# Perceiver attention on one core: context preparation over five pairs, and a table load placed after the square roots

## The chip, the cores and the metric

One core of a Trainium2 chip (trn2). The metric is device time in microseconds (us), the median of the runs shown; the profile describes one further execution of the same program. TensorE does the matrix products, VectorE (DVE) and ScalarE (ACT) the elementwise work, GpSimd (POOL) a part of the normalisation, and SyncE (SP) issues the transfers.

## The reference

Four residual steps run one after the other on x, of shape 8 x 100 x 512: a perceiver cross attention, a mixture of experts (4 experts, two per token), a strided cross attention and a second mixture of experts (8 experts, two per token), each scaled by tanh of a gate. The change lies in the first step alone:

```python
xn = layernorm(x, ln_x_g, ln_x_b)            # x: the context rows, 8 x 722 x 512
ln = layernorm(latents, ln_l_g, ln_l_b)      # latents: layernorm of x, 8 x 100 x 512
q = ln @ Wq                                  # 16 heads of 64
kv = concatenate((xn, ln), axis=1) @ Wkv     # 822 keys and values per batch
sim = where(mask, (q * scale) @ k.T, -max)
out = softmax(sim) @ v                       # per head
out = layernorm(out @ Wout, ln_o_g, ln_o_b)
```

## The kernel before

`perceiver_attention` (line 59) goes through 8 batches, and in each through 8 pairs of heads (index `i` for the batch, `hp` for the pair, `n = 8 i + hp`). Each engine has its own instruction stream, written out by hand in the same loop order, and the streams meet only in semaphores. There is no planner: the order in which TensorE works is the order in which the loops at lines 797 to 832 issue.

One turn of TensorE, pair n: the scores of pair n (`scores`, 690), the attention product of pair n-2 (`attend`, 717), then in alternation the transposes of pair n-1's probabilities (`transposes`, 705) and the keys of pair n+1 (`keys`, 673), and at the end the *extras* of the pair (`extras`, 241). Extras are tiles of two kinds. A *values tile* ("v") is 12 products of 512 columns into one PSUM bank, which ScalarE copies to `v_sb` (515). A *context tile* ("in") is 4 transposes of 128 normalised context rows of the next batch into one PSUM bank (637); ScalarE copies the high part out (497) and VectorE writes the low part (883), and only then is the bank free. Twelve values tiles and six context tiles are needed per batch. The first four values tiles of a batch are made in the last two pairs of the batch before (`NEXT`), the rest in its own pairs (`OWN`; `FIRST_OWN` for batch 0). `PREP` says how many context tiles of the next batch each pair makes. Within a pair the two kinds alternate, values first (253).

Keys, values and context tiles share two PSUM banks (`kv_ps`), which are handed out in strict turns: each use takes the other bank than the use before it, and `wait_kv` (624) makes TensorE wait until the use before last has been read out. So a context tile behind one values tile waits for the second part of the keys, whose bank VectorE frees with `k_lo` (900); a context tile right behind another context tile waits for ScalarE's copy of the values tile before both.

ScalarE's stream of one pair (584 to 609) is: `move_t` of the first transposes (533), high keys part 0 (526), `move_t` of the second, `exponent` of head 0 (543), high keys part 1, `exponent` of head 1, at pairs 0 and 2 a square root (`deviations`, 489), then the copies of the extras. TensorE's second round of transposes waits for the first `move_t`, since both use the bank `t_ps`. The square root at pair 0 is for the next batch's context rows, the one at pair 2 (from batch 1 on) for the output of the batch before; in the last batch there is one more at pair 5. A square root and an exponential need different activation tables; the compiler puts an ACT_TABLE_LOAD ahead of the first activation that needs the other table. The copies need neither.

VectorE's stream of one pair (1027 to 1076): at pair 1 it takes the reciprocal of the deviations and normalises the first three context tiles, at pair 2 the other three, at pair 3 it finishes the output of the batch before (`finish`, 944); then `move_o` (927), `move_t` (920), the maximum and division of both heads, the low keys (900) between them, and the low parts of the pair's context tiles. GpSimd multiplies and adds gain and bias to each normalised context tile (461, 462), and TensorE's context tile waits for that. SyncE loads the rows of batch i+2 once the last context tile of batch i+1 has been transposed (430).

Of the kernel before, what the change touches and what calls it, by code (L numbers as in the profile page):

```python
# [8 lines left out]
ACT = mybir.ActivationFunctionType  # L9
# [49 lines left out]
def perceiver_attention(nc, ctx_rows, x_in, keep_mask, ln_x_g, ln_x_b, ln_l_g, ln_l_b, wq, wkv, wout,  # L59
# [5 lines left out]
    B, M, D = x_in.shape  # L65
    N = ctx_rows.shape[1]
    P = 128
# [28 lines left out]
    with ExitStack() as ctx:  # L96
        def sb(name, shape, dt=F32, where=ctx):
            return where.enter_context(nc.sbuf_tensor("a_" + name, shape, dt))
# [47 lines left out]
        eps = sb("eps", [P, 1])  # L146
        ident = sb("ident", [P, P])
        stats = sb("stats", [P, CT + 2, 6])
        mean_var = sb("mean_var", [P, CT + 2, 2])
        std = sb("std", [P, CT + 2])  # L150
        rstd = sb("rstd", [P, CT + 2])
        l_stats = sb("l_stats", [P, B, 6])
# [79 lines left out]
        pool_chain = sem("pool_chain")  # L232

        halves = (slice(0, HD), slice(HD, P))
        OWN = [2, 1, 2, 1, 1, 1, 0, 0]
        FIRST_OWN = [4, 3, 2, 1, 1, 1, 0, 0]
        NEXT = [0, 0, 0, 0, 0, 0, 2, 2]
        PREP = [0, 0, 0, 2, 2, 2, 0, 0]
        P_FROM = [sum(PREP[:hp]) for hp in range(PAIRS)]

        def extras(i, hp):

            own = OWN if i else FIRST_OWN
            first = VS - sum(own[hp:])
            vs = [("v", i, v) for v in range(first, first + own[hp])]
            if i + 1 < B:
                first = sum(NEXT[:hp])
                vs += [("v", i + 1, v) for v in range(first, first + NEXT[hp])]
            ins = [("in", i + 1, t) for t in range(P_FROM[hp], P_FROM[hp] + PREP[hp]) if i + 1 < B]
            both = []  # L250
            if (i, hp) == (0, 0):
                both = [("tail", u) for u in range(TAILS)]
            while vs or ins:
                both += vs[:1] + ins[:1]
                vs, ins = vs[1:], ins[1:]
            return both

        def turned(i, hp):

            return [j for j, at in ((i - 2, 1), (i - 1 if i == B - 1 else -1, 7)) if j >= 0 and hp == at]  # L260
# [220 lines left out]
        def _(act):  # L481
# [3 lines left out]
            def deviations(first, end):  # L485

                dev[0] += 1
                act.wait_ge(var_done, dev[0])
                nc.scalar.activation(std[:, first:end], mean_var[:, first:end, 1], ACT.Sqrt, bias=eps[:, :]).then_inc(std_done, 1)
# [31 lines left out]
            def keys(n, part):  # L521
                c, w = PART[part]
                act.wait_ge(k_ready, 2 * n + part + 1)
                if n:
                    act.wait_ge(s_ready, 2 * n)
                nc.scalar.activation(k_hi[:, c:c + w], kv_bank("k", n, part)[:, 0:w], ACT.Copy).then_inc(k_hi_done, 1)  # L526

            def move_t(n, x):
                a, b = ROUND[0]
                act.wait_ge(t_ready, 4 * n + 2 * x + 1)  # L530
                if n:
                    act.wait_ge(o_ready, n)
                nc.scalar.activation(probs_t[:, x, M * a:M * b], t_ps[:, 0:M * (b - a)], ACT.Copy).then_inc(ta_done, 1)  # L533

            def move_next(b):
                act.wait_ge(xt_ready, b + 1)
                if b:
                    act.wait_ge(routed, b)
                nc.scalar.activation(xn_t[:, :, :], turn_bank(b).rearrange("p (k q) -> p k q", q=P)[:, :, 0:M], ACT.Copy).then_inc(turn_sem(b), 1)

            def exponent(n, x):
                act.wait_ge(max_done, 2 * n + x + 1)
                nc.scalar.activation(probs[0:M, x, 0:KEYS], probs[0:M, x, 0:KEYS], ACT.Exp, scale=-1.0,  # L543
                                     bias=neg_max[0:M, x:x + 1], accum_out=row_sum[0:M, x:x + 1]).then_inc(exp_done, 1)
# [39 lines left out]
            for i in range(B):  # L584
                for hp in range(PAIRS):
                    n = PAIRS * i + hp
                    if n:
                        move_t(n - 1, 0)
                    if n + 1 < PAIRS * B:
                        keys(n + 1, 0)  # L590
                    if n:
                        move_t(n - 1, 1)
                    exponent(n, 0)
                    if n + 1 < PAIRS * B:
                        keys(n + 1, 1)
                    for j in turned(i, hp):
                        move_next(j)
                    exponent(n, 1)
                    if hp == 0:
                        if i + 1 < B:  # L600
                            deviations(0, CT + 1)
                        else:
                            deviations(NEXT_IN, NEXT_IN + 1)
                    if hp == 2 and i:
                        deviations(OUT, OUT + 1)
                    if hp == 5 and i == B - 1:
                        deviations(NEXT_IN, NEXT_IN + 1)
                    for kind, *at in extras(i, hp):
                        {"v": values, "in": prepare, "tail": tail_values}[kind](*at)
            move_t(PAIRS * B - 1, 0)  # L610
            move_t(PAIRS * B - 1, 1)
            deviations(OUT, OUT + 1)
# [1938 lines left out]
def flamingo_layers(nc, x, ctx_1024, mask_BxS2_bk0, g_xattn, g_ffn,  # L2551
# [11 lines left out]
    with ExitStack() as ctx:  # L2563
        logits = ctx.enter_context(nc.sbuf_tensor("logits", [P, B * m_wg_t.shape[1]], F32))
        route1 = RoutingAhead(nc, "f", ctx, x.shape, f_router_w, f_router_b, logits)
        route2 = RoutingAhead(nc, "m", ctx, x.shape, m_wg_t, None, logits)
        gates = ctx.enter_context(nc.sbuf_tensor("gates", [P, B, TOP], F32))
        with nc.cleanup_on_exit():
            perceiver_attention(nc, ctx_1024, x, mask_BxS2_bk0, a_ln_x_g, a_ln_x_b, a_ln_l_g, a_ln_l_b, a_wq, a_wkv, a_wout,
                                a_ln_o_g, a_ln_o_b, g_xattn[0:1], x1, route1)  # L2570

        least = -(-B * M * TOP // P)
        even = m_wg_t.shape[1] * -(-B * M * TOP // m_wg_t.shape[1] // P)
        with nc.cleanup_on_exit(), ExitStack() as held:
            rows_at = held.enter_context(nc.sbuf_tensor("f_rows_at", [P, 2, slots(B * M, f_router_b.shape[0])], mybir.dt.uint32))
            with ExitStack() as early:
                tensors = ExpertTensors(nc, "f", early, B, B * M, D, f_router_b.shape[0], least + least % 2, False)
            ahead = ContextAhead(nc, held, (tensors.wab_hi, tensors.wab_lo, tensors.x_hi, tensors.x_lo), B, B * M, g_ctx, g_wk_t, g_wv_t)
            with ExitStack() as early:
                sums = SumsAhead(nc, early, ahead, rows_at, x1, y1, least + least % 2)  # L2580
            with nc.cleanup_on_exit():
                gated_experts(nc, "f", x1, route1, f_pieces, g_ffn[0:1], gates, y1, None, least + least % 2, tensors, ahead, sums)
            strided_attention(nc, x1, y1, gates, ahead, sums, g_wq_t, g_bias, g_wo_t, g_bo, g_xattn[1:2], x3, route2)
        with nc.cleanup_on_exit():
            gated_experts(nc, "m", x3, route2, m_pieces, g_ffn[1:2], gates, y2, out, even)
# [57 lines left out]
```

## Time and profile before

| | us |
|---|---|
| median of 3 runs | 2108.15 |
| lowest and highest run | 2107.41, 2115.01 |
| span of the profiled execution | 2099.3 |
| TensorE busy in the span | 1928.3 (92%) |
| VectorE, ScalarE, GpSimd busy | 1026.6, 845.0, 657.1 |

The span goes from the first to the last instruction. The profile gives no other time for that execution; the runs shown lie 8.1 to 15.7 us above the span, for what is outside it. The eight batches of the perceiver lie between about 110 and 1060 us; the three later stages follow.

### The profile page before, as it was taken

The page shows a single profiled execution, that of the slowest core. Times are in us where ns is not written, and L with a number is a line of the kernel's source. Part 1 is how long each engine was busy: PE and PEld are TensorE (multiplying, and loading weights), DVE is VectorE, ACT ScalarE, POOL GpSimd, SP SyncE. Part 2 cuts the span into 40 slices and gives each one's busy share as a digit, 9 for nine tenths or more (in the row PEclk, how much of TensorE's full clock was granted, in tenths as well). Part 3 has the DMA queues.
Part 4 walks back from the last instruction along what each step waited for, and adds up shares of the span by engine and source line. Part 5 has one row for each costly group of instructions (what it writes and reads, how often), then busy time and mean ns, then how long its engine had stood idle before and what let it go on. Part 6 is the DMA issues. An engine that isn't in the chain of part 4 may idle for free. (4 is left out here: it accounts for less than half of the span.)

```text
span 2099.3 us, 35633 instructions
## 1 busy us (share of the span) xinstructions
PE 1928.3 (92%) x12328; PEld 1568.3 (75%) x12328; DVE 1026.6 (49%) x2245; ACT 845.0 (40%) x1792; POOL 657.1 (31%) x551
## 2 busy tenths in 40 slices
PE   4889999999999999999859999999997895999994
PEld 3577878777777878787748888888885675999983
DVE  6324555555555555544464233333336566554564
ACT  3233443444434434334435233333322544555550
POOL 4011020303020110300023455554433204688872
PEclk9899999999999999999969999999998996999997
DMA  7630101010110201000044233333348216454546
GB/s 209 200 130 1 53 15 53 19 53 11 37 35 9 63 9 53 19 17 18 5 152 137 57 110 110 105 110 120 109 143 263 101 58 202 147 200 152 209 146 202
DMA packets 113526, 201.58 MB, mean 96 GB/s; under 512 B 33135, under 2 KB 33935, under 8 KB 112867
## 3 DMA queue, kind: packets, MB, share of 16 engines
q1 hardware_dynamic: 108579, 183.94, 27.3%
q0 software_dynamic: 4800, 15.73, 2.3%
q8 instruction: 86, 1.41, 0.3%
q14 instruction: 61, 0.50, 0.1%
HBM read 171.65 MB, written 27.99 MB: 95 GB/s over the span
## 5 line engine op out<-in xcount | busy, mean ns | idle before, releaser
L461 POOL TENSOR_TENSOR a_rows<-a_rows,a_gain_x 128x512 f32<-128x512 f32 (+1 forms) x48 | 69.3, 1443 | 555.7 <-DVE a_rows L876 555.7
L620 PE MATMUL a_kv_ps<-a_kvin_hi,a_wk_hi 128*128 128x512 f32 (+1 forms) x512 | 196.0, 383 | 1.0 <-DVE a_kvin_lo L883 1.0
L1094 PE MATMUL f_banks<-f_wab_hi,f_x_hi 128*128 x448 | 183.8, 410 | 0.7 <-DVE f_x_lo L1781 0.7
L621 PE MATMUL a_kv_ps<-a_kvin_lo,a_wk_hi 128*128 128x512 f32 (+1 forms) x512 | 180.3, 352 | 0.0
L622 PE MATMUL a_kv_ps<-a_kvin_hi,a_wk_lo 128*128 128x512 f32 (+1 forms) x512 | 180.2, 352 | 0.0
L1096 PE MATMUL f_banks<-f_wab_hi,f_x_lo 128*128 x448 | 176.8, 395 | 0.0
L1095 PE MATMUL f_banks<-f_wab_lo,f_x_hi 128*128 x448 | 176.1, 393 | 0.0
L543 ACT ACTIVATE a_probs<-a_probs,a_neg_max 100x822 f32<-100x822 f32 x128 | 125.9, 984 | 113.1 <-DVE a_neg_max L907 112.9
L1803 DVE TENSOR_TENSOR f_h_sb<-f_h_sb,f_banks 128x256 f32<-128x256 f32 x112 | 47.2, 421 | 240.6 <-ACT f_h_sb L1526 239.6
L1526 ACT ACTIVATE f_h_sb<-f_banks 128x256 f32<-128x256 f32 x112 | 43.1, 385 | 290.5 <-PE f_banks L1096 290.5
L620 PE MATMUL a_kv_ps<-a_wv_hi,a_kvin_hi 128*128 128x512 f32 (+1 forms) x384 | 156.6, 408 | 1.0 <-DVE a_k_lo L900 1.0
L1094 PE MATMUL m_banks<-m_wab_hi,m_x_hi 128*128 x512 | 154.4, 302 | 1.6 <-DVE m_x_lo L1781 0.9
L622 PE MATMUL a_kv_ps<-a_wv_hi,a_kvin_lo 128*128 128x512 f32 (+1 forms) x384 | 152.1, 396 | 0.0
L621 PE MATMUL a_kv_ps<-a_wv_lo,a_kvin_hi 128*128 128x512 f32 (+1 forms) x384 | 151.4, 394 | 0.0
L533 ACT ACTIVATE a_probs_t<-a_t_ps 128x400 f32<-128x400 f32 x128 | 64.3, 503 | 208.9 <-PE a_t_ps L714 208.9
L1096 PE MATMUL m_banks<-m_wab_hi,m_x_lo 128*128 x512 | 145.8, 285 | 0.0
L1095 PE MATMUL m_banks<-m_wab_lo,m_x_hi 128*128 x512 | 145.3, 284 | 0.0
L526 ACT ACTIVATE a_k_hi<-a_kv_ps 128x512 fp32r<-128x512 f32 (+1 forms) x128 | 65.5, 512 | 174.6 <-PE a_kv_ps L622 168.3
L920 DVE COPY a_probs_t<-a_t_ps 128x300 f32<-128x300 f32 x128 | 59.9, 468 | 153.1 <-PE a_t_ps L714 153.1
L907 DVE CUSTOM_DVE_ANT_0 a_probs<-a_s_ps,a_mask_add 100x822 f32<-100x822 f32 x128 | 128.6, 1005 | 0.0
L1464 POOL TENSOR_TENSOR f_wy_lo<-f_raw,f_wy_hi 128x512 fp32r<-128x512 f32 x60 | 77.4, 1289 | 157.3 <-ACT f_wy_hi L1503 157.3
L714 PE MATMUL a_t_ps<-a_ident,a_probs 100*128 100x100 f32 x896 | 122.9, 253 | 0.7 <-DVE a_probs_t L920 0.7
(411 smaller groups left out, 4874.9 us busy)
## 6 DMA issues: line engine op xcount, KB each, us to landing
f_raw<-f_pieces SPq DMA_DIRECT2D x94, 256.0 KB, 2.7
m_raw<-m_pieces SPq DMA_DIRECT2D x92, 256.0 KB, 2.9
f_wab_raw<-f_pieces SPq DMA_DIRECT2D x42, 512.0 KB, 6.2
m_wab_raw<-m_pieces SPq DMA_DIRECT2D x42, 512.0 KB, 6.6
a_rows<-ctx SPq DMA_DIRECT2D x8, 1280.0 KB
ahead_piece<-g_ctx SPq DMA_DIRECT2D x2, 2880.0 KB, 20.1
a_wout_sb<-L_xattn_Wkv SPq DMA_DIRECT2D x8, 512.0 KB, 14.6
m_y_acc<-m_pieces SPq DMA_DIRECT2D x8, 512.0 KB, 5.9
```

What stands on the lines that cost most here:

```text
L461: own.link(nc.gpsimd.tensor_tensor(row, row, gain_x[0:n, :], ALU.mult))
L526: nc.scalar.activation(k_hi[:, c:c + w], kv_bank("k", n, part)[:, 0:w], ACT.Copy).then_inc(k_hi_done, 1)
L543: nc.scalar.activation(probs[0:M, x, 0:KEYS], probs[0:M, x, 0:KEYS], ACT.Exp, scale=-1.0, bias=neg_max[0:M, x:x + 1], accum_out=row_sum[0: ...
L620: nc.tensor.matmul(out, hi_l, hi_r, start=first, stop=False)
L621: nc.tensor.matmul(out, hi_l, lo_r, start=False, stop=False)
L622: return nc.tensor.matmul(out, lo_l, hi_r, start=False, stop=last)
L714: ins = nc.tensor.transpose(t_ps[:, M * (t - a):M * (t - a) + M], probs[0:M, x, KFROM[t]:KFROM[t] + P], ident[0:M, 0:M])
L907: nc.vector.tensor_tensor_reduce(out=probs[0:M, x, 0:KEYS], in0=s_ps[0:M, x, 0:KEYS], in1=mask_add[0:M, :], scale=-1.0, scalar=3.0e38, op0 ...
L1094: nc.tensor.matmul(out, left_hi, right_hi, start=start, stop=False)
L1095: nc.tensor.matmul(out, left_hi, right_lo, start=False, stop=False)
L1096: return nc.tensor.matmul(out, left_lo, right_hi, start=False, stop=stop)
L1464: nc.gpsimd.tensor_tensor(split_dst(wab_lo, wy_lo, c), raw_of(q, n), split_dst(wab_hi, wy_hi, c).bitcast(F32), ALU.subtract).then_inc(wlo_ ...
```

## The change

Three lines and one small tile. The six context tiles of the next batch, which were made two at a time in pairs 3, 4 and 5, are made one at a time in pairs 1 to 4 and two in pair 5. One values tile moves from pair 2 to pair 5 in batches 1 to 7; batch 0 keeps its own list. After the extras of pairs 0 and 2 of every batch, ScalarE takes one exponential of a 128x1 constant into a column that nothing reads.

```diff
+        unread = sb("unread", [P, 2 * B])
...
-        OWN = [2, 1, 2, 1, 1, 1, 0, 0]
+        OWN = [2, 1, 1, 1, 1, 2, 0, 0]
         FIRST_OWN = [4, 3, 2, 1, 1, 1, 0, 0]
         NEXT = [0, 0, 0, 0, 0, 0, 2, 2]
-        PREP = [0, 0, 0, 2, 2, 2, 0, 0]
+        PREP = [0, 1, 1, 1, 1, 2, 0, 0]
...
                     for kind, *at in extras(i, hp):
                         {"v": values, "in": prepare, "tail": tail_values}[kind](*at)
+                    if hp in (0, 2):
+                        c = 2 * i + hp // 2
+                        nc.scalar.activation(unread[:, c:c + 1], eps[:, :], ACT.Exp)
```

With this the extras of batches 1 to 6 go, pair by pair, from v v, v, v v, v in in, v in in, v in in, v v, v v to v v, v in, v in, v in, v in, v in v in, v v, v v. In batch 0, pairs 1 to 5 go from v v v, v v, v in in, v in in, v in in to v in v v, v in v, v in, v in, v in in. In batch 7, which prepares nothing, pair 2 has one values tile instead of two and pair 5 two instead of one.

## Rows read from the trace of the kernel before

**Rows 1.** Windows view: busy us (instructions) by engine, granted clock, DMA
```profile
520.00:630.00 110.00, 107.51 (x784) 85.30 (x783) 58.80 (x133) 44.90 (x84) 17.20 (x13) 1.00 0.12 34
```

**Rows 2.** The waits view of TensorE, 180 to 1060: us in total, times, longest
```profile
PE a_kv_ps L637 <- ACT a_v_sb L515: 8.5, 21, 0.6
PE a_kv_ps L637 <- DVE a_k_lo L900: 5.9, 6, 1.0
PE a_s_ps L700 <- DVE a_k_lo L900: 4.6, 2, 3.7
PE a_o_ps L729 <- DVE logits L970: 1.4, 5, 0.3
```

**Rows 3.** Timeline, TensorE, batch 3, pair 4: start, us, instruction, count, [idle before]
```profile
550.61 0.60 PE L637 MATMUL a_kv_ps<-a_ident,a_rows 128*128 128x128 f32 x4
551.55 0.63 PE L637 MATMUL a_kv_ps<-a_ident,a_rows 128*128 128x128 f32 x4 [0.34 <-ACT a_v_sb L515]
552.11 0.47 PE L700 MATMUL a_s_ps<-a_k_hi,a_q_hi 64*100 64x512 f32 x2
```

**Rows 4.** Timeline of TensorE, batch 3, end of pair 5
```profile
563.77 0.60 PE L637 MATMUL a_kv_ps<-a_ident,a_rows 128*128 128x128 f32 x4
564.72 0.47 PE L637 MATMUL a_kv_ps<-a_ident,a_rows 82*128 82x82 f32 x4 [0.34 <-ACT a_v_sb L515]
```

**Rows 5.** Timeline of TensorE, batch 4, end of pair 3
```profile
651.57 0.40 PE L622 MATMUL a_kv_ps<-a_wv_hi,a_kvin_lo 128*128 128x512 f32 x1
652.97 0.63 PE L637 MATMUL a_kv_ps<-a_ident,a_rows 128*128 128x128 f32 x4 [1.00 <-DVE a_k_lo L900]
654.17 0.63 PE L637 MATMUL a_kv_ps<-a_ident,a_rows 128*128 128x128 f32 x4 [0.57 <-ACT a_v_sb L515]
654.72 0.48 PE L700 MATMUL a_s_ps<-a_k_hi,a_q_hi 64*100 64x512 f32 x2
```

**Rows 6.** Timeline of VectorE, batch 3, pair 5, then batch 4, pair 3
```profile
562.89 0.47 DVE L900 TENSOR_TENSOR a_k_lo<-a_kv_ps,a_k_hi 128x310 fp32r<-128x310 f32 x1
...
652.35 0.48 DVE L900 TENSOR_TENSOR a_k_lo<-a_kv_ps,a_k_hi 128x310 fp32r<-128x310 f32 x1
```

**Rows 7.** Timeline of ScalarE, batch 4, pairs 2 and 3
```profile
637.96 1.28 ACT L489 ACT_TABLE_LOAD   x1
639.25 0.29 ACT L489 ACTIVATE a_std<-a_mean_var,a_eps 128x1 f32<-128x1 f32 x1
639.46 0.58 ACT L515 ACTIVATE a_v_sb<-a_kv_ps 128x512 f32<-128x512 f32 x1
640.61 0.60 ACT L515 ACTIVATE a_v_sb<-a_kv_ps 128x512 f32<-128x512 f32 x1 [0.58 <-PE a_kv_ps L622]
643.76 0.51 ACT L533 ACTIVATE a_probs_t<-a_t_ps 128x400 f32<-128x400 f32 x1 [2.56 <-PE a_t_ps L714]
...
647.87 1.28 ACT L543 ACT_TABLE_LOAD   x1
```

**Rows 8.** Timeline of TensorE, batch 4, from pair 2 into pair 3
```profile
637.40 0.39 PE L622 MATMUL a_kv_ps<-a_wv_hi,a_kvin_lo 128*128 128x512 f32 x1
...
640.50 0.48 PE L700 MATMUL a_s_ps<-a_k_hi,a_q_hi 64*100 64x512 f32 x2
...
643.16 0.56 PE L714 MATMUL a_t_ps<-a_ident,a_probs 100*128 100x100 f32 x4
...
644.98 0.42 PE L714 MATMUL a_t_ps<-a_ident,a_probs 100*128 100x100 f32 x3
```

**Rows 9.** Timeline of ScalarE, batch 4, start of pair 1
```profile
610.96 0.51 ACT L533 ACTIVATE a_probs_t<-a_t_ps 128x400 f32<-128x400 f32 x1 [2.56 <-PE a_t_ps L714]
```

**Rows 10.** Timeline of GpSimd, batch 4: second pass, first context tile
```profile
610.11 1.28 POOL L462 TENSOR_TENSOR a_rows<-a_rows,a_bias_x 128x512 f32<-128x512 f32 x1
```

**Rows 11.** Timeline of TensorE, batch 7: scores of pair 4, attention in pair 6
```profile
1001.98 0.48 PE L700 MATMUL a_s_ps<-a_k_hi,a_q_hi 64*100 64x512 f32 x2 [0.86 <-DVE a_k_lo L900]
...
1028.22 1.42 PE L729 MATMUL a_o_ps<-a_probs_t,a_v_sb 128*64 128x100 f32 x28 [1.30 <-ACT a_v_sb L515]
```

## The prediction

> **What bounds the kernel now.** I read the stage first, with the windows view over 110 us of the perceiver's eight batches. TensorE is busy for 107.51 of 110 us, at granted clock 1.00, the 2.4 GHz level; VectorE, ScalarE and GpSimd are at half or less, and DMA at 0.12 [rows 1]. TensorE's order sets the time there. Its products don't change in number or size, so the change can only win or lose the time in which TensorE waits. The waits view lists that time: 8.5 us in 21 waits of context tiles (line 637) for ScalarE's copy of a values tile, 5.9 us in 6 waits of the same line for VectorE's low keys, 4.6 us in two waits of the scores, and 1.4 us in five waits for the logits [rows 2]. Then I read the timelines around one place of each kind.
>
> In pair 4 the first context tile starts at 550.61 and the second at 551.55, 0.94 later, with 0.34 idle put down to the values copy; the scores start 0.56 after the second [rows 3]. Nothing holds that second tile's end, so a tile with nothing to wait for takes at most 0.56. As the switch to another kind of product is in it, I take 0.46 (an estimate, 0.1 either way). Pair 4 so loses 0.94 - 0.46 = 0.48. Pair 5 has 0.95 between its tiles, a loss of 0.49 [rows 4].
>
> Pair 3 is worse. A values tile needs 0.24 per product (640.50 - 637.40 = 3.10 for 13 steps [rows 8]), so the one of pair 3 ends at 651.57 + 0.24 = 651.81. The first context tile starts at 652.97, 1.16 late, and the second another 1.20 later, 0.74 more than it needs: 1.90 in all [rows 5]. The cause is on ScalarE: after the square root of pair 2 the exponential of pair 3 needs a table load of 1.28 [rows 7], and that delay goes through the division and the next maximum to VectorE's low keys, whose bank the tile takes. In pair 5, without a load, the low keys end at 562.89 + 0.47 = 563.36, 0.41 ahead of the tile at 563.77; in pair 3 at 652.83, 1.02 behind the values tile [rows 4 to 6].
>
> **The change part by part.**
>
> *Context tiles spread.* In batches 1 to 6 pairs 1 to 4 get one context tile behind one values tile. It takes the bank of the low keys, and those end 0.41 early when no load delays them. The tile then waits for no values copy. Pair 5 has v in v in: its second values tile comes behind a context tile and waits for the first values copy just as the second context tile does now, so one 0.49 stays. Its last context tile waits for a bank that has a whole values tile (12 x 0.24 = 2.9) to come free. Saved: 1.90 + 0.48 + 0.49 - 0.49 = 2.38 per batch, times 6 = 14.3. That includes the load's part of pair 3. If the idle time of the trace is all that is lost, it is 1.00 + 0.57 + 0.34 = 1.91, times 6 = 11.5; if a tile needs 0.36, it is 15.5.
>
> Batch 0 gains nothing: it has three such waits now, in pairs 3, 4 and 5, and three after, two values tiles behind a context tile in pairs 1 and 2 and the two context tiles in a row in pair 5.
>
> *Earlier tiles, other engines.* The first context tile of pair 1 needs GpSimd's scaled rows. They are ready at 610.11 + 1.28 = 611.39 [rows 10]. Pair 1's first move is at 610.96 [rows 9], and from that move to the end of the values tile pair 3 takes 651.81 - 643.76 = 8.05 [rows 5, 7], so the tile is due near 619.0: 7.6 to spare, and cost 0. In batch 0 the copy of that tile also waits for the query stores (line 495), two pairs earlier than now; pair 0 alone has twelve tiles, 12 x 2.9 = 35 us, to hide them, so 0. SyncE's rows for batch i+2 wait for the sixth context tile, which is still the last extra of pair 5 with the same products ahead of it, so the load is not later.
>
> *Unread exponentials.* There are 16, each 0.29 by the square root of the same shape, and 15 of them carry a load of 1.28 that now stands at the next pair's first exponential: 1.57 on ScalarE, ahead of the next `move_t`. Behind pair 0 ScalarE is idle for 2.56 ahead of that move [rows 9]: hidden, with 1.0 left. Behind pair 2 it is tight. The pair now ends in a context tile instead of a values tile, so the scores start at 637.40 + 0.24 + 0.56 = 638.20, 2.30 earlier [rows 3, 8], and the move is due at 643.76 - 2.30 = 641.46. ScalarE runs: values copy to 639.46 + 0.58 = 640.04, context copy about 0.58 more, load 1.28, exponential 0.29: 642.2, some 0.7 late [rows 7]. TensorE's second round of transposes comes at 644.98, 0.71 after the move's end at 643.76 + 0.51 = 644.27 [rows 7, 8]. So the lateness is just covered; I take 0. The ends are a gain of nothing and a loss of 0.2 x 7 = 1.4. If that cover were gone, 0.7 x 7 = 4.9 would show. VectorE has the tile's low part more to do there ahead of `finish` and `move_o`, about the 0.48 of a low key part [rows 6]; the next reader of `move_o` is TensorE a pair later, so 0, at worst 0.48 x 6 = 2.9.
>
> *Batch 7.* Pair 3's load holds the scores of pair 4 for 0.86; the exponential removes it. The attention product of pair 6 waits 1.30 for the last values copy, which pair 5's square root delays [rows 11]; with two values tiles in pair 5 ScalarE has 2.9 more before the last, so this goes too: 2.2 together. The longer wait, 4.6 - 0.86 = 3.7 [rows 2], comes from the square root of pair 5 and stays, since no unread exponential follows it.
>
> *Logits.* They are late by 0.3 in five batches [rows 2] behind the context tiles of pair 4. With one tile TensorE arrives 0.94 earlier, and VectorE has a copy and a low part fewer ahead of it. I take 0.1 more each, 0.4 in all; between 0 and (0.94 - 0.48) x 5 = 2.3.
>
> **Sum.** 14.3 + 2.2 - 0.4 = 16.1 us off the profiled execution's span of 2099.3, so 2083.2. The median of the runs is 2108.15, 8.85 above that span, for what lies around it; I take that as unchanged: 2092.0. The later stages start when this one is done, and I let them shift as they are; a few transfers and clock steps may fall otherwise, for which I allow 2 either way. With the ends above (11.5 + 2.2 - 2.3 - 1.4 = 10.0 and 15.5 + 2.2 = 17.7) the forecast's own range is 2090 to 2098.
>
> **The rivals.**
>
> *The load is not moved, or moves nothing.* If the load still stands at the next pair's exponential, pair 1's new tile waits as pair 3's does now, and only the spreading counts: pair 3 loses 1.16, pair 5 0.49, pair 1 about 0.7 (its low keys are 1.02 behind, and the transposes of the turned rows ahead of the tile take some 0.3): 2.35 against 2.87, so 0.5 x 6 and the 1.3 of batch 7: 4.3, which gives 2103.9. For it speaks that the result is unread. Against it: the loads in the trace stand directly ahead of the activation that needs them [rows 7]. Chance 0.08.
>
> *A switch takes longer than its record.* If a load kept ScalarE for a second 1.28, the move behind pair 2 would be 0.7 + 1.28 = 2.0 late, 1.3 beyond its cover, in seven batches 9; behind pair 0 it would be 0.3 late and covered. Gain 16.1 - 9 = 7.1: 2101.1. Against it: the load starts at 637.96, ends at 639.24, and the square root starts at 639.25 [rows 7]. Chance 0.06. The Trainium skill states such a rule ("ScalarE: Activation LUTs", section "What ACT_TABLE_LOAD costs"): a load of some 1283 ns and with it a drain of about 1380 ns, 2.66 us for every switch. The trace agrees on the load and shows no drain in front of it or behind it. By the page the move would be 2.1 late, and the time, an estimate, near 2102.
>
> *ScalarE becomes the bound at the pair's head: slower.* The load and exponential stand between the last copy and the `move_t` on which TensorE's transposes depend. If all 15 were exposed in full, TensorE would lose 15 x 1.57 = 23.6, more than the gain: 2108.15 - 16.1 + 23.6 = 2115.7. It decides from 16.1 / 15 = 1.1 exposed each. For it speaks that pair 2 has nothing left by my sum; against it the idle 2.56 ahead of both moves now [rows 7, 9]. Chance 0.04.
>
> **How the numbers follow.** The forecast has 0.77, the three rivals 0.08, 0.06 and 0.04, and 0.05 is for a smaller gain by something I don't see. A measurement of this kernel tells about 0.5% (10.5 us) from no change: faster means below 2097.6. The forecast falls there but for its last end, with part of the 0.05; both smaller gains are within 0.5%; of the third rival, 7.5 us above before, I count 0.03 beyond 0.5%, since the waits would also move VectorE: faster 0.79, same 0.18, slower 0.03. The range goes from 2087 (the forecast's low end with luck behind it) to 2101, to the second rival.
>
> **What would show it.** The waits view should have no wait of line 637 for low keys; its 21 waits for the values copy should fall to one (batch 0, pair 5), with eight new ones of about the same length at line 620, where a values tile follows a context tile. Batch 7 keeps only the wait of 3.7. Square roots keep their loads, the exponential of line 543 has one load left in this stage instead of sixteen, and the new line has fifteen, ended ahead of `move_t`. A new wait of line 714 for ScalarE's `move_t` would show that pair 2 lacks its cover. I am wrong if context tiles still wait in pairs 1 to 4, or if the perceiver ends less than 10 us earlier.

## The result, and the profile after

The changed kernel takes 2097.49 us (median of 5 runs, 2094.27 to 2100.29). On the same chip the kernel before took 2115.01 (5 runs, 2107.41 to 2117.75). The ratio is 0.9931, with the interval 0.9914 to 0.9948: 0.7% faster, 14.6 us by the ratio (the two medians alone differ by 17.5). The forecast was 2092.0, a gain of 16.1 off the median of three runs that was known then, 2108.15. The profiled execution has a span of 2095.8 us and takes 2097.49.

Here are the waits of TensorE between 180 and 1060 us (microseconds in all, times, longest), the view of [rows 2]:

```profile
...
PE a_s_ps L704 <- DVE a_k_lo L904: 3.8, 1, 3.8
PE a_kv_ps L641 <- DVE a_k_lo L904: 3.1, 5, 0.7
...
PE a_o_ps L733 <- DVE logits L974: 1.7, 5, 0.3
PE a_kv_ps L624 <- ACT a_v_sb L516: 1.5, 6, 0.3
...
PE a_kv_ps L641 <- ACT a_v_sb L516: 0.3, 1, 0.3
```

Lines are 1 to 4 higher than before: the context tiles' 637 is now 641, the values and keys' 620 is 624, the low keys' 900 is 904, the values copy's 515 is 516. Of the 21 waits of context tiles for a values copy [rows 2] one of 0.3 is left, in batch 0, and six short ones of line 624 stand in this stretch instead (two more lie ahead of it, in batch 0). Both counts are as predicted. Of the two waits of the scores the one of 3.8 is left. What wasn't to be there is the wait of line 641 for line 904: five context tiles still wait 0.6 to 0.7 for low keys. (Ahead of these stands one wait of 4.6, of line 752 for the last batch's output; before, that one came later than 1060.)

ScalarE in batch 4, behind pair 0 and behind pair 2 (start, duration, instruction, idle before), against [rows 7, 9]:

```profile
601.16 0.60 ACT L516 ACTIVATE a_v_sb<-a_kv_ps 118x512 f32<-118x512 f32 x1 [0.59 <-PE a_kv_ps L626]
601.78 1.28 ACT L613 ACT_TABLE_LOAD   x1
603.07 0.20 ACT L613 ACTIVATE a_unread<-a_eps 128x1 f32<-128x1 f32 x1
604.32 0.51 ACT L534 ACTIVATE a_probs_t<-a_t_ps 128x400 f32<-128x400 f32 x1 [1.04 <-PE a_t_ps L718]
...
634.34 1.28 ACT L613 ACT_TABLE_LOAD   x1
635.63 0.20 ACT L613 ACTIVATE a_unread<-a_eps 128x1 f32<-128x1 f32 x1
635.74 0.49 ACT L534 ACTIVATE a_probs_t<-a_t_ps 128x400 f32<-128x400 f32 x1
```

The loads stand where the exponentials are. Behind pair 0 there is 1.04 of idle left ahead of the move, behind pair 2 none. Loads by line, 100 to 1060 us (count, then busy us and mean ns): the exponentials of line 544 have one left of sixteen, the new line has fifteen.

```profile
L490 ACT ACT_TABLE_LOAD x17 | 21.8, 1283 | 0.3
L613 ACT ACT_TABLE_LOAD x15 | 19.2, 1283 | 0.3
...
L544 ACT ACT_TABLE_LOAD x1 | 1.3, 1283 | 0.0
```

The context tile of pair 3 in batch 4, which was 1.16 late in [rows 5], on TensorE:

```profile
643.04 0.40 PE L626 MATMUL a_kv_ps<-a_wv_hi,a_kvin_lo 128*128 128x512 f32 x1
644.10 0.63 PE L641 MATMUL a_kv_ps<-a_ident,a_rows 128*128 128x128 f32 x4 [0.66 <-DVE a_k_lo L904]
644.66 0.48 PE L704 MATMUL a_s_ps<-a_k_hi,a_q_hi 64*100 64x512 f32 x2
```

The values tile ends at 643.04 + 0.24 = 643.28, so this tile is 0.82 late. What holds it is on VectorE and GpSimd; first VectorE, then GpSimd:

```profile
640.52 1.73 DVE L917 TENSOR_SCALAR a_probs<-a_probs,a_row_inv 100x822 f32<-100x822 f32 x1
642.17 0.46 DVE L924 COPY a_probs_t<-a_t_ps 128x300 f32<-128x300 f32 x1
...
643.48 0.47 DVE L904 TENSOR_TENSOR a_k_lo<-a_kv_ps,a_k_hi 128x310 fp32r<-128x310 f32 x1
```

```profile
640.52 1.29 POOL L474 TENSOR_TENSOR a_res<-a_res,a_bias_o 100x512 f32<-100x512 f32 x1 [17.17 <-DMA a_res<-x_rolled]
```

The first division of pair 3 (line 917) takes 1.73. The second takes 0.65, as all divisions did before, when none overlapped with an instruction of GpSimd. GpSimd's add of the bias to the next residual rows (line 474) starts at the same moment. The division ends at 642.25, 0.44 behind the add's end at 641.81. That is so in five batches of this profile, whatever the start: the divisions take 1.70 to 1.75 and end 0.44 to 0.45 behind the add. In batch 3 the add comes at 527.62, behind the division at 526.68 (0.65), and there is no wait. The Trainium skill states such a lock ("SBUF — State Buffer", section "Who interferes with whom"): VectorE's tensor_scalar in a two-port mode and a GpSimd instruction share one pair of ports, and the second waits until the first is done. The trace agrees: 0.65 became 1.73 beside an add that kept its 1.29.

The same happens in a second place. The exponential behind pair 0 brings the first division of pair 1 forward, to where GpSimd adds the bias to context rows (line 463), in batches 2 to 6; in batch 4, VectorE and then GpSimd:

```profile
609.62 0.83 DVE L917 TENSOR_SCALAR a_probs<-a_probs,a_row_inv 100x822 f32<-100x822 f32 x1
```

```profile
608.71 1.30 POOL L463 TENSOR_TENSOR a_rows<-a_rows,a_bias_x 128x512 f32<-128x512 f32 x1
```

The five divisions take 0.77 to 0.84 and end 0.45 behind that add. No context tile of pair 1 waits for it, so it cost TensorE nothing that the waits show.

To see where the 16 us are, I cut the spans at the start of the scores of each batch's pair 0 and at VectorE's first instruction of the next stage (the handover). "Before, again" is the second profile of the kernel before, from the experiments.

| us | before | before, again | after | after, again |
|---|---|---|---|---|
| up to the first scores | 100.54 | 102.07 | 99.97 | 101.98 |
| batch 0 | 145.33 | 145.25 | 144.93 | 144.05 |
| batches 1 to 6 | 696.55 | 696.52 | 686.05 | 685.84 |
| batch 7 to the handover | 129.48 | 128.27 | 124.98 | 127.08 |
| later stages | 1027.39 | 1041.19 | 1039.83 | 1041.16 |
| span | 2099.3 | 2113.3 | 2095.8 | 2100.1 |

From the first scores to the handover the changed kernel is 13.1 to 15.4 us shorter. Most of that scatter lies behind the scores of pair 7 of batch 7, where the twelve profiles of this study take 30.2 to 32.5 whatever the kernel; up to those scores batch 7 takes 96.9 before and 94.6 after. In batch 0 it lies in pair 0 (47.0 to 48.4); the pairs behind it go from 97.8 to 96.6. Behind the handover it looks 12.4 us longer than the profile before the prediction, but not than the second one.

### The profile page after: what moved, and what is told of

Read it like the earlier page. It is cut to its first block and busy times, and to the rows that moved or that the text cites. A ratio compares the mean times of both kernels' runs of the same rounds, so it can differ in the third digit from the quotient of the medians.

```text
span 2095.8 us, 35637 instructions
## 1 busy us (share of the span) xinstructions
PE 1930.7 (92%) x12328; PEld 1571.3 (75%) x12328; DVE 1032.9 (49%) x2245; ACT 845.0 (40%) x1808; POOL 657.4 (31%) x551
## 6 DMA issues: line engine op xcount, KB each, us to landing
a_wout_sb<-L_xattn_Wkv SPq DMA_DIRECT2D x8, 512.0 KB, 14.5
```

## The experiments

The kernel before took 2113.21 on the chip of the first four experiments, and 2115.69 on that of the second profile of before, the copies, the five exponentials and the version further. Lengths are those of the table's stretches.

**The changed kernel again**, no edit.

> The changed kernel again, unaltered. In its first profile the perceiver hands over to the experts (VectorE's first f_scratch) at 1055.9 us, against 1071.9 in the profile of before; 12.5 of these 16.0 us are lost behind it, 7.5 of them in one idle stretch of ScalarE near 1766. Theory A (the stages behind vary from execution to execution): the handover is again within 1 us of 1055.9, and the stages behind take another time than 1039.9, with other idle stretches. Theory B (the change itself makes the stages behind slower, for its 16 more ScalarE instructions or the shift): the same stretches of about 4, 5 and 8 us stand at the same places, and the time behind the handover is again near 1040. The ratio to before is 0.993 by either.

2102.55 (2097.10 to 2104.96), ratio 0.9945 (0.9931 to 0.996). The five long divisions (1.60 to 1.72) and the five waits for low keys (2.8 in all) are there again. By the ratio the gain is 11.6 here. Neither theory fits whole: the handover comes at 1058.94, 3.0 later, and the stages behind take 1041.19, near 1040 as theory B has it. The second profile of before (below) decides between them. The gain up to the handover is stable in batches 1 to 6 (685.84 and 686.05) and varies by 2 us behind them.

**The exponentials alone.**

```diff
-        OWN = [2, 1, 1, 1, 1, 2, 0, 0]
+        OWN = [2, 1, 2, 1, 1, 1, 0, 0]
...
-        PREP = [0, 1, 1, 1, 1, 2, 0, 0]
+        PREP = [0, 0, 0, 2, 2, 2, 0, 0]
```

> The unread exponentials alone; the context tiles stay two at a time in pairs 3 to 5, and the values tiles as before. By the forecast's steps pair 3 loses as little as pair 4 (0.5 instead of 1.9), 1.4 in six batches, and the scores of pair 4 in batch 7 don't wait (0.9): 9.3 us at the handover, near 1062.6. The waits of context tiles for low keys go from 6 to 0, those for the values copy stay 21. The rival (the load is not the cause, the two tiles in a row are): handover near 1071. If 16 more ScalarE instructions bring the idle stretches behind the handover, they are here too.

2104.87, ratio 0.996 (0.9948 to 0.9972). Batches 1 to 6 take 688.16, 8.4 less than before, and batch 0 takes 143.89, 1.4 less; the waits for low keys in front of context tiles are gone, and the 21 for the values copy stay, at 7.2. No division of pair 3 is long: the add comes at 639.67 in batch 4, with none within 2 us of it. (The five of pair 1 are, 0.77 to 0.83.) The handover is at 1060.07, 2.5 earlier than expected; the theory had nothing for batch 0.

**The spreading alone.**

```diff
...
-                    if hp in (0, 2):
-                        c = 2 * i + hp // 2
-                        nc.scalar.activation(unread[:, c:c + 1], eps[:, :], ACT.Exp)
```

> The context and values tiles dealt as in the change, without the exponentials. By the forecast's steps pair 1 loses 0.7, pair 3 1.2 and pair 5 0.5, so 0.5 gained in six batches and 1.3 in batch 7: 4.3 us at the handover, near 1067.6; twelve waits of context tiles for low keys. The rival (the dealing alone does it, the load only follows): near 1058. If ScalarE's 16 more instructions bring the idle stretches behind the handover, they are absent here.

2110.91, ratio 0.9989 (0.9978 to 1.0001). Batches 1 to 6 take 694.99, 1.5 less; from the first scores to the handover it gains 3.8 against the second profile of before and 5.1 against the first. Its waits of context tiles:

```profile
PE a_kv_ps L637 <- DVE a_k_lo L900: 10.6, 12, 1.5
```

Two tiles per batch, those of pairs 1 and 3, now wait for low keys behind a load. So the two parts are worth 8.4 and 1.5 in batches 1 to 6, less than the 14.5 that both give where nothing collides (below): a tile spread to a pair with a load gains only where that load has gone.

**The add held back.** GpSimd waits until the divisions of pair 3 are done; nothing is left out.

```diff
                 pool.wait_ge(res_loaded, 16 * (b + 1))
+                pool.wait_ge(p_done, 2 * (PAIRS * b + 3) + 2)
```

> The change, with GpSimd's addition of the output bias to the residual held until the divisions of pair 3 are done. In the changed kernel that addition starts within 0.1 us of VectorE's first division of pair 3 in five batches; that division takes 1.70 to 1.75 instead of 0.65, and the context tile of pair 3 waits 0.7 for the low keys. Theory (GpSimd's addition stretches the division): all divisions of pair 3 take 0.65, the five waits for low keys are gone, the handover is 3.5 to 4 us earlier, near 1052. Rival (the division is late for VectorE's own order, since finish comes later): they stay, near 1056.

2095.89, ratio 0.9919 (0.9903 to 0.9936). Batch 4, on VectorE, GpSimd and TensorE in turn:

```profile
639.46 0.65 DVE L918 TENSOR_SCALAR a_probs<-a_probs,a_row_inv 100x822 f32<-100x822 f32 x1
...
641.33 0.47 DVE L905 TENSOR_TENSOR a_k_lo<-a_kv_ps,a_k_hi 128x310 fp32r<-128x310 f32 x1
```

```profile
643.54 1.28 POOL L475 TENSOR_TENSOR a_res<-a_res,a_bias_o 100x512 f32<-100x512 f32 x1 [21.28 <-DVE a_probs L918]
```

```profile
641.98 0.39 PE L627 MATMUL a_kv_ps<-a_wv_hi,a_kvin_lo 128*128 128x512 f32 x1
642.21 0.60 PE L642 MATMUL a_kv_ps<-a_ident,a_rows 128*128 128x128 f32 x4
642.74 0.47 PE L705 MATMUL a_s_ps<-a_k_hi,a_q_hi 64*100 64x512 f32 x2
```

The division takes 0.65 again, and the context tile follows its values tile with no wait. Against the changed kernel's lengths, batch by batch:

| us, batch | 1 | 2 | 3 | 4 | 5 | 6 |
|---|---|---|---|---|---|---|
| before | 115.03 | 116.26 | 116.36 | 116.26 | 116.36 | 116.28 |
| after | 113.32 | 114.70 | 113.95 | 114.71 | 114.69 | 114.68 |
| add held back | 112.56 | 113.88 | 113.95 | 113.84 | 113.95 | 113.84 |

Batch 3 is unchanged and the five others are 0.74 to 0.87 shorter, 4.0 together. With the add out of the way every batch gains 2.4 (mean 2.42 against the first row); the forecast had 2.38. Pair by pair it is the forecast's sum too: in batch 4 pair 3 is 2.39 shorter (1.90 lost and 0.46 for a tile: 2.36), pair 4 0.98 shorter (0.48 and 0.46: 0.94), and pairs 1, 2 and 5 together, between which a values tile and two context tiles move, 0.94 longer (two context tiles: 0.92).

**The kernel before, profiled again**, no edit.

> The kernel before, unchanged, for a second profile of it. Theory A: the later stages take longer in the executions of this set of runs whatever the kernel, and the 2099.3 us profile of before was a quick execution. Then the profiled span is 2108 to 2114, VectorE's first f_scratch comes at 1071.9 +- 1 (the perceiver doesn't vary), some 1036 to 1048 lie behind it instead of 1027.4, and ScalarE shows the idle stretches of 4 to 8 us with no semaphore near 1100 and 1760 to 1790 and the nine of 1.8. Theory B: the change makes the later stages longer. Then the span is near 2099, 1027 lie behind the handover and none of those stretches is there. Ratio 1.000 either way.

2115.67, ratio 1.0002 (0.9991 to 1.0012), span 2113.3. Handover at 1072.11, later stages 1041.19. Here are windows of 25 us at the start of the last stage (busy us and instructions of TensorE, its weight load, VectorE, ScalarE and GpSimd; granted clock; DMA): the profile before the prediction, the second one, and the changed kernel.

```profile
1757.00:1782.00 25.00, 19.43 (x124) 18.24 (x125) 16.86 (x39) 9.01 (x23) 17.84 (x18) 0.76 0.63 186
```

```profile
1762.00:1787.00 25.00, 14.96 (x66) 13.08 (x67) 13.55 (x30) 4.34 (x11) 15.85 (x16) 0.64 0.58 168
```

```profile
1745.00:1770.00 25.00, 15.30 (x68) 13.42 (x69) 13.49 (x30) 4.34 (x11) 15.82 (x16) 0.64 0.57 169
```

The second and the third are alike: 66 and 68 matmuls, clock 0.64. The first has 124 at clock 0.76 (both are means over stretches at 1.2 and at 2.4 GHz). ScalarE stands in this stretch, in the second profile of before and in the changed kernel, and the profile doesn't tell what ended its wait ("remote"):

```profile
1783.46 0.28 ACT L1526 ACTIVATE m_h_sb<-m_banks 128x128 f32<-128x128 f32 x1 [8.01 <-remote]
```

```profile
1766.00 0.28 ACT L1530 ACTIVATE m_h_sb<-m_banks 128x128 f32<-128x128 f32 x1 [7.93 <-remote]
```

In the other profiles of this study one such idle time of 5.0 to 8.8 lies at this place, whatever the kernel; only the profile before the prediction has none, and its later stages take 1027.39 where the eleven others have 1036.7 to 1047.7. So the 12.4 us are not the change's doing. What keeps ScalarE there is open.

**Copies in place of the exponentials.**

```diff
-                        nc.scalar.activation(unread[:, c:c + 1], eps[:, :], ACT.Exp)
+                        nc.scalar.activation(unread[:, c:c + 1], eps[:, :], ACT.Copy)
```

> The changed kernel with a copy in place of each unread exponential: the same 16 instructions in the same places, but no table load in them, so the loads stay at the next pair's exponential. If the load's place is what the exponentials are worth, this falls back to the spreading alone: context tiles wait for low keys about 10 us in 12 waits, the handover comes near 1069, the ratio is near 0.999. If an extra instruction there is what counts (another order of ScalarE's work), the handover stays near 1056 to 1059 and the ratio near 0.994.

2113.06, ratio 0.9989 (0.9977 to 1.0), batches 1 to 6 at 694.84, 0.15 from the spreading alone. Its waits are the same too:

```profile
PE a_kv_ps L641 <- DVE a_k_lo L904: 10.6, 12, 1.5
```

The same instructions without a load are worth nothing. What counts is the place of the load.

**Five exponentials for one**, on the changed kernel.

```diff
...
-                        nc.scalar.activation(unread[:, c:c + 1], eps[:, :], ACT.Exp)
+                        for k in range(5):
+                            nc.scalar.activation(unread[:, 5 * c + k:5 * c + k + 1], eps[:, :], ACT.Exp)
```

> The changed kernel with five unread exponentials in each place instead of one, to measure the cover. Four more take 0.44 to 0.8 (the next instruction starts 0.11 behind the start of one whose record is 0.20). Behind pair 0 ScalarE has 1.04 idle left, so nothing. Behind pair 2 the move ends at 636.23 and TensorE's second transposes come at 636.45, 0.2 of cover: 0.24 to 0.6 too late in seven batches, 1.7 to 4.2 in all, and new waits of the transposes (line 718) for ScalarE's move; the handover comes at 1057.6 to 1063. If there is more cover than I read, the handover stays at 1056 to 1059 and line 718 has no new wait.

2104.76, ratio 0.9953 (0.9938 to 0.9968). The handover comes at 1059.11, and no new wait of the transposes shows. Of the cover this says nothing: batches 1, 2 and 4 to 6 keep their length (114.70 for 114.71 in batch 4), because the division there ends by the add's end and not by its own start. In batch 4 (GpSimd, then VectorE):

```profile
641.94 1.29 POOL L474 TENSOR_TENSOR a_res<-a_res,a_bias_o 100x512 f32<-100x512 f32 x1 [17.20 <-DMA a_res<-x_rolled]
```

```profile
642.18 1.50 DVE L918 TENSOR_SCALAR a_probs<-a_probs,a_row_inv 100x822 f32<-100x822 f32 x1
```

It starts 0.24 behind the add instead of with it, takes 0.23 less, and ends 0.45 behind it again. In batch 3 the later division now meets the add (1.79), and that batch goes from 113.95 to 115.01.

**Five and ten exponentials with the add held back** (one run each).

> GpSimd's bias add held until the divisions of pair 3 are done, with five unread exponentials in each place: the cover behind pair 2 without the collision on top of it. Five took 0.58 us in one record (with one: 0.20), so the move behind pair 2 comes 0.38 later. With the held add and one exponential it ends at 634.68 + 0.49 = 635.17, and TensorE's second transposes come at 635.38: 0.21 of cover. If that is all the cover, TensorE loses 0.17 in each of batches 1 to 6, and the batch lengths (start of the scores of pair 0 to the next) go from 113.84-113.95 to 114.0-114.1. If the tiles behind give the loss back, they stay at 113.84-113.95.

> The same with ten unread exponentials: some 0.87 more than one behind pairs 0 and 2. Behind pair 0 there is 1.04 of idle ahead of the move: nothing. Behind pair 2 with 0.21 of cover TensorE waits 0.66 longer, so the batch lengths go to 114.5-114.6. If there is cover behind the transposes that I don't read (as much as the 0.66 that the tiles have until the next wait), they stay near 113.9.

Times 2090.41 and 2096.53, beside 2118.9 for before. The batch lengths tell it: with one, five and ten exponentials batch 4 takes 113.84, 114.10 and 114.56. Five further ones cost 0.46, their full length: ten have a record of 1.04, five of 0.57. The first four cost 0.26 of their 0.37, so one exponential leaves about 0.1 of cover behind pair 2; I expected 0.21. With ten the wait shows at the transposes of seven batches:

```profile
PE a_t_ps L720 <- ACT a_probs_t L535: 3.3, 7, 0.5
```

**A version further:** the add held back, and one more unread exponential behind pair 5's extras in batch 7.

```diff
...
-                    if hp in (0, 2):
-                        c = 2 * i + hp // 2
+                    if hp in (0, 2) or (i, hp) == (B - 1, 5):
+                        c = 2 * i + min(hp, 4) // 2
```

> The changed kernel with GpSimd's bias add held until VectorE's divisions of pair 3 are done, and one more unread exponential behind the extras of pair 5 in batch 7. If the wait of 3.7 of the scores there is a table load of 1.28 in a chain ScalarE, VectorE, TensorE, it falls to about 2.4 and the handover comes at 1052.3 - 1.3 = 1051.0; time about 1.3 below the kernel with the held add alone, 2095. Rival: the load now stands ahead of the next move, which TensorE's transposes wait for, and what the scores gain the transposes lose: the handover stays at 1052.3. In both the five divisions of 1.7 and the waits of context tiles for low keys stay away.

2094.56, ratio 0.9917 (0.9894 to 0.994). The scores' wait in batch 7 falls from 3.7 to:

```profile
PE a_s_ps L705 <- DVE a_k_lo L905: 2.3, 1, 2.3
```

Up to the scores of pair 7 batch 7 goes from 94.63 to 93.20, 1.4 less; 1.3 was expected. That is too little for the times to tell it from the add held back alone (0.9919), and less than what varies behind pair 7.

## Why the prediction was right or wrong

*Where the time goes: right.* The time was won where TensorE waited in the perceiver, and by both parts together. The exponentials' worth lies in the load, as the copies show. That the time came into the range is in part luck: the gain was 14.6 and in the repeat 11.6 instead of 16.1, and the repeat's 2102.55, on another chip, lies above the range's 2101. What the profiles show as stable is 14.0: 1.2 in batch 0, 10.5 in batches 1 to 6, 2.3 in batch 7.

*Context tiles, 2.38 per batch: right in its mechanism, wrong in the sum.* Batch 3, and all six with the add held back, gained 2.4. The other five of the changed kernel gained 1.55 to 1.71. Batches 1 to 6 so gave 10.5 instead of 14.3.

*The step that failed* is "the next reader of `move_o` is TensorE a pair later, so 0, at worst 0.48 x 6 = 2.9", with `finish` ahead of it. I followed only `move_o` to its reader, and took the lengths of VectorE's instructions as given. The end of `finish` frees the residual rows: their load follows, and then GpSimd's add. Before, in batch 4, the end of `finish` and the first division of pair 3 on VectorE, then the add on GpSimd:

```profile
640.57 0.75 DVE L950 SCALAR_TENSOR_TENSOR a_tail<-a_tail,a_rstd,a_res 100x512 f32<-100x512 f32 x1
...
650.48 0.65 DVE L913 TENSOR_SCALAR a_probs<-a_probs,a_row_inv 100x822 f32<-100x822 f32 x1
```

```profile
645.11 1.28 POOL L473 TENSOR_TENSOR a_res<-a_res,a_bias_o 100x512 f32<-100x512 f32 x1 [14.86 <-DMA a_res<-x_rolled]
```

After, the end of `finish`:

```profile
635.93 0.75 DVE L954 SCALAR_TENSOR_TENSOR a_tail<-a_tail,a_rstd,a_res 100x512 f32<-100x512 f32 x1
```

In the changed kernel `finish` ends at 636.68 and the add comes 3.84 later; before, it took 3.79. But the first division of pair 3 came 9.2 behind `finish` then (the load of [rows 7] and the second values tile stood between) and now comes 3.84 behind it. The change brought the two together; price 4.0 in five batches, 0.8 each. The streams so meet not only in semaphores, as the description of the kernel has it: this collision is in no semaphore and in no wait of VectorE. The prediction named "context tiles still wait in pairs 1 to 4" as a sign that it would be wrong, and that is what the waits show.

*Unread exponentials, 0: right.* Pair 0 has 1.04 left (forecast 1.0). An exponential takes 0.20, not 0.29, and the move starts 0.11 behind its start. So the move behind pair 2 is about 0.5 late, not 0.7 (it starts at 635.74; TensorE's first transposes start at 634.63, and before the move followed them by 0.60). About 0.1 of cover is left. No drain shows: the load of 634.34 ends at 635.62, and the next activation starts at 635.63. So the second rival falls. The Trainium skill's drain of about 1380 ns ("ScalarE: Activation LUTs", section "What ACT_TABLE_LOAD costs") is not to be seen in this trace.

*Batch 0, 0: a miss.* One of its values tiles, in pair 1, waited 1.0 for low keys behind a load (at 159.18; the load at 154.08). I had read the waits from 180 us only. The gain was 1.2, behind pair 0; the exponentials alone give it too.

*Batch 7, 2.2: right.* Its 0.86 and 1.30 are gone and 3.8 stays. Up to the scores of pair 7 it gained 2.3 in both profiles; the stretch to the handover gained 1.2 to 4.5, by the scatter behind them.

*Logits, 0.4: right in sign.* 1.4 became 1.7.

*The later stages, "let them shift as they are", and "8.85 above that span, for what lies around it": wrong.* The changed kernel has 1.7 around its span, and so has the second profile of before (2115.02 and 2113.3). The 8.85, and the 8.1 to 15.7 named with the profile before, were no time around the span: the profiled execution was quicker in its later stages than the second profile, by the 13.8 that the table shows. The forecast for the time survives it, since I took the gain off the median. The span of 2083.2 doesn't; it is 12.6 longer. And the 2 either way that I allowed for these stages are not in the forecast's own range: 2090 to 2098 is 10.0 and 17.7 off the median.

*The rivals.* The load moves, and it costs its record; ScalarE isn't the bound. The first rival's 4.3 for spreading alone was close to the 3.8 to 5.1 of that run, but partly by luck: its 1.3 for batch 7 holds (1.3 up to the scores of pair 7), its 3.0 for batches 1 to 6 measured 1.5, and the rest is scatter. Pair 1 lost 0.84 there instead of 0.7, and in batch 3 the add met a division (1.21) and cost 0.6.

## What to carry to other kernels

When a load or an extra instruction moves a stretch of work, list the transfers and GpSimd work that the same stretch sets free, and see what they now meet on VectorE: an off-path add of 1.29 cost 0.8 in each of five batches on the path, and one more wait in front of it took that away. No view of waits shows it on VectorE, where the record is only longer; look for instructions of one form and unequal length. A single profiled execution can be quicker than the median in a stage that the change doesn't touch: take a difference off the median, and compare stage by stage. An instruction that only moves a table load is worth what its load was on the path, less what the next reader of that engine lacks in cover.

## What the runs showed of the hardware that I had not expected

A VectorE division of 100x822 and a GpSimd add of 100x512 don't share the time. The division took 1.19 to 1.79 instead of 0.65 and ended 0.44 to 0.45 behind the add, whether it began up to 0.56 behind the add or 0.04 ahead of it by the records; so their starts don't tell which of the two has to wait. Beside GpSimd's add of 128x512 it is the same with a start 0.9 to 1.0 behind it; a division that began 1.2 behind an add kept its 0.65. The add kept its 1.28 to 1.31 each time. A 128x1 activation takes 0.20 alone, and ten in a row take 1.04.

ScalarE stood for 5.0 to 8.8 us at the entry of the last stage, in all profiles but one, and the profile doesn't tell what ended the wait.
